# One-byte counts in the third layer of a graph network kernel

## The reference

```
x = layernorm(x + segment_sum(x[src] @ W[edge_type], dst))       # first layer
x = layernorm(x + segment_sum(x[src] * edge_weight, dst))        # second
x = layernorm(x + segment_sum(x[src], dst))                      # third
x = layernorm(x + tensor-product messages of an MLP, summed)     # fourth
```

## Time and profile before

| | us |
|---|---|
| median of three runs | 6759.45 |
| profiled execution, own time | 6756.3 |
| its span | 6754.5 |
| PE matmul busy | 5258.6 (78%) |
| PE weight loads | 4062.3 (60%) |
| DVE busy | 3937.8 (58%) |
| ACT busy | 2910.4 (43%) |
| POOL busy | 4128.8 (61%) |
| chain that ended last | POOL 59%, issue 19%, DMA 15%, PE 4% |

### The profile page before, as it was taken

How to read it: one execution, slowest core, us unless ns; L and a number is a source line. 1 busy time by engine, 2 the same in 40 slices (tenths; PEclk the granted TensorE clock), 3 DMA queues, 4 the chain that set the end, 5 groups by cost and what they waited for, 6 DMA issues and landing times.

```text
span 6754.5 us, 124961 instructions
## 1 busy us (share of the span) xinstructions
PE 5258.6 (78%) x43024; PEld 4062.3 (60%) x43025; DVE 3937.8 (58%) x7842; ACT 2910.4 (43%) x7150; POOL 4128.8 (61%) x4168
## 2 busy tenths in 40 slices
PE   6777777776777766755556769999999999999997
PEld 3367767776666666721112436777776777777766
DVE  4366666666666666620001027777777777777777
ACT  4444434343443433410000016666666666666665
POOL 0677777777777777710000027777777777777774
PEclk8555555555555555567667977787878777777877
DMA  8744444444444444489999961111111111111111
GB/s 270 265 164 175 172 164 164 173 173 164 164 164 172 175 164 164 180 325 386 387 387 378 387 211 28 27 27 27 27 27 27 27 27 28 28 28 27 27 27 20
DMA packets 512177, 1005.50 MB, mean 149 GB/s; under 512 B 180257, under 2 KB 247906, under 8 KB 478306
## 3 DMA queue, kind: packets, MB, share of 16 engines
q1 hardware_dynamic: 289890, 453.14, 19.4%
q10 hardware_dynamic: 88800, 475.02, 17.8%
q0 software_dynamic: 133120, 71.57, 6.5%
HBM read 521.51 MB, written 476.05 MB: 148 GB/s over the span
## 4 chain that ended last, share of the span: by engine, by line
POOL 59%; issue 19%; DMA 15%; PE 4%; ACT 1%; DVE 1%; POOLq 0%; SPq 0%; ACTq 0%; DVEq 0%
POOL gathered L506 59%; DMA arena<-adj 9%; DMA arena<-counts 4%; PE psum L710 2%; PE psum L884 1%; PE psum L888 1%; DMA rel_table<-arena 1%; ACT table_out L542 0%; PE psum L736 0%; PE psum L767 0%; DMA rel_table<-table_out 0%; ACT arena L542 0%; DMA arena<-in_L_gnn_weight 0%; PE psum L949 0%; DMA arena<-arena 0%
## 5 line engine op out<-in xcount | busy, mean ns | idle before, releaser
L506 POOL DMA_INDIRECT gathered<-x_rows,idx x2048 | 2065.5, 1009 | 1725.8 <-issue 1725.8
L506 POOL DMA_INDIRECT gathered<-rel_table,idx x2048 | 1998.0, 976 | 632.1 <-issue 632.1
L591 ACT COPY arena<-psum 128x512 f32<-128x512 f32 x1024 | 604.2, 590 | 1580.6 <-PE psum L817 1551.1
L949 PE MATMUL psum<-w,arena 65*128 65x256 f32 x4096 | 1231.8, 454 | 2.3 <-DVE arena L1392 2.3
L949 PEld LDWEIGHTS psum<-w,arena 65*128 65x128 f32 x4096 | 914.9, 231 | 301.3 <-issue 130.0
L817 PE MATMUL psum<-arena 64*128 64x64 bf16 (+1 forms) x12288 | 534.8, 254 | 536.7 <-DVE arena L1188 497.0
L767 PE MATMUL psum<-gathered,arena 128*128 128x32 f32 x4096 | 826.2, 380 | 150.1 <-DMA gathered<-rel_table,idx 148.1
L767 PEld LDWEIGHTS psum<-gathered,arena 128*128 128x128 f32 x4096 | 815.2, 309 | 165.1 <-issue 151.7
L767 PE MATMUL psum<-arena 128*128 128x184 f32 x4096 | 895.8, 379 | 3.4 <-DVE acc L1217 3.4
L767 PEld LDWEIGHTS psum<-arena 128*128 128x128 f32 x4096 | 861.1, 237 | 40.6 <-issue 3.9
L817 PEld LDWEIGHTS psum<-arena 64*128 64x128 bf16 x12288 | 494.1, 120 | 577.4 <-issue 561.2
(11 more groups left out here) (173 smaller groups left out, 5339.8 us busy)
## 6 DMA issues: line engine op xcount, KB each, us to landing
adj<-arena ACTq DMA_DIRECT2D x128, 2048.0 KB
arena<-adj SPq DMA_DIRECT2D x128, 2048.0 KB, 19.8
counts<-arena ACTq DMA_DIRECT2D x128, 1024.0 KB
arena<-counts SPq DMA_DIRECT2D x64, 2048.0 KB, 20.0
rel_table<-table_out ACTq DMA_DIRECT2D x16, 2048.0 KB, 7.5
rel_table<-arena ACTq DMA_DIRECT2D x16, 2048.0 KB, 7.6
gathered<-rel_table,idx POOLq DMA_INDIRECT x2048
arena<-in_edge_attr SPq DMA_DIRECT2D x128, 256.0 KB
```

The costliest lines, as they stand in the source:

```text
L506: pool.indirect_dma_start(gathered[:, s, j, :], None, rows[l], bass.IndirectOffsetOnAxis(ap=idx[:, s, j:j + 1], axis=0),).then_inc(rows_in ...
L591: act.copy(w_to, made[:, 0]).then_inc(w_out, 1)
L949: mm = pe.matmul(pair[g % 2][:, WN * q:WN * q + WN], hidden[:, s % 2, q, P * g:P * g + P], w2[:, :], start=True, stop=True)
```

## The change

`counts` is stored in one byte per entry: ACT casts to the 8-bit float format `float8e4`, the stores and loads move the bytes as `uint8`, and PE reads them as `float8e4`. A load of 2 MB then holds 32 of the 64 `high` values, so there are 32 loads. The slots are also checked for repeated sources: `prepare_slots` compares each slot's source with those 1 to 4 places further on and sums the matches in each lane and round; the dense path is taken only if no lane has more than four. The pad records get distinct sources for this. The arena shrinks by 768 columns.

```
-        counts = nc.dram_tensor("counts", [CHUNKS, P, HIS, STRIP_D], F16).ap()
+        counts = nc.dram_tensor("counts", [CHUNKS, P, HIS, STRIP_D], U8).ap()
-        ARENA = 27904
+        ARENA = 27136
+        repeats = sb("repeats", [P, ROUNDS + 1])
+        slot_same = sb("slot_same", [P, REPEATS, 2, SLOT])
-        SLOT_LINKS, TAKE_LINKS = 8, 7
+        SLOT_LINKS, TAKE_LINKS = 11, 7
# load_strips (SP)
-                matrix, his = ((adj, SUPER), (counts, 2 * SUPER))[l - 1]
+                matrix, his = ((adj, SUPER), (counts, COUNT_HI))[l - 1]      # COUNT_HI = 32
-                    to = load_in[k] if l == 1 else load_in[k].bitcast(F16)
+                    to = load_in[k] if l == 1 else load_in[k].bitcast(U8)
# strip_rows (ACT)
-                    act.copy(c_to, made[:, 1]).then_inc(c_out, 1)
+                    act.copy(c_to, made[:, 1], saturate=False).then_inc(c_out, 1)
# end of the first layer (PE)
-            pe.transpose(bank_slot[0:1, 0:P], found_col[:, :], ident[:, :]).then_inc(found_turned, 1)
+            for k in range(2):
+                pe.transpose(bank_slot[0:1, P * k:P * k + P], found_col[:, k:k + 1], ident[:, :]).then_inc(found_turned, 1)
# dense_strips (PE)
-                        part_in = load_in[at] if l == 1 else load_in[at].bitcast(F16)
+                        part_in = load_in[at] if l == 1 else load_in[at].bitcast(F8)
-                dense_strips(2, 2 * SUPER)
+                dense_strips(2, COUNT_HI)
# setup (DVE)
-            dve.memset(pad[:, :], -1.0).then_inc(packed, 1)
+            dve.memset(pad[:, 1:2], -1.0)
+            dve.tensor_scalar(pad[:, 0:1].bitcast(I32), part_i[0:SLOT, :], -1.0, -1.0, ALU.mult, ALU.add
+                              ).then_inc(packed, 1)
+            dve.memset(slot_same[:, :, :, :], 0.0)
# prepare_slots (DVE), behind its last operation
+                slots_made(dve.tensor_scalar(slot_i[:, 0], words, NODES - 1, None, ALU.bitwise_and), due(9))
+                for k in range(1, REPEATS + 1):
+                    same = dve.tensor_tensor(slot_same[:, k - 1, :, 0:SLOT - k], slot_i[:, 0, :, 0:SLOT - k],
+                                             slot_i[:, 0, :, k:SLOT], ALU.is_equal)
+                slots_made(same, due(10))
+                slots_made(dve.tensor_reduce(repeats[:, bass.ds(q, 1)],
+                                             slot_same[:, :, :, :].rearrange("p k b s -> p (k b s)"), AX.X, ALU.add), due(11))
# end of the first layer (DVE)
-            dve.tensor_reduce(found_col[:, :], found[:, 0:ROUNDS], AX.X, ALU.add).then_inc(found_ready, 1)
-            dve.wait_ge(found_turned, 1)
+            dve.tensor_reduce(found_col[:, 0:1], found[:, 0:ROUNDS], AX.X, ALU.add)
+            dve.tensor_reduce(found_col[:, 1:2], repeats[:, 0:ROUNDS], AX.X, ALU.max).then_inc(found_ready, 1)
+            dve.wait_ge(found_turned, 2)
+            link(dve.tensor_reduce(found_row[:, 1:2], bank_slot[0:1, P:2 * P], AX.X, ALU.max))
+            link(dve.tensor_scalar(found_row[:, 3:4], found_row[:, 1:2], float(REPEATS), None, ALU.is_le))
...
```

More of the change, by code:

```diff
@@ L24 @@
 LOADS = 6
+COUNT_HI = 32
+REPEATS = 4
 ALU = mybir.AluOpType
@@ L30 @@
 BF16 = mybir.dt.bfloat16
-F16 = mybir.dt.float16
+F8 = mybir.dt.float8e4
+U8 = mybir.dt.uint8
 AX = mybir.AxisListType
@@ L153, in build @@
         found = sb("found", [P, ROUNDS + 1])
-        found_row = sb("found_row", [1, P + 2])
-        found_col = sb("found_col", [P, 1])
+        found_row = sb("found_row", [1, 4])
+        found_col = sb("found_col", [P, 2])
+        repeats = sb("repeats", [P, ROUNDS + 1])
+        slot_same = sb("slot_same", [P, REPEATS, 2, SLOT])
         dense_ok = sb("dense_ok", [1, 1], I32)
@@ L171, in build @@
         stage_w = [cut(HIS * STRIP_D).rearrange("p (h d) -> p h d", d=STRIP_D) for _ in range(2)]
-        stage_c = [cut(HIS * STRIP_D // 2).bitcast(F16).rearrange("p (h d) -> p h d", d=STRIP_D) for _ in range(2)]
+        stage_c_at = [cut(HIS * STRIP_D // 4) for _ in range(2)]
+        stage_c = [a.bitcast(F8).rearrange("p (h d) -> p h d", d=STRIP_D) for a in stage_c_at]
+        stage_bytes = [a.bitcast(U8).rearrange("p (h d) -> p h d", d=STRIP_D) for a in stage_c_at]
         half_cols = HALF_D * (P + 4 * HIS) // 2
         half_at = [table_out[:, :, :].rearrange("p a b -> p (a b)")[:, 0:half_cols], cut(half_cols)]
-        assert taken[0] == ARENA - 2 * TILES * P
+        assert taken[0] <= ARENA - 2 * TILES * P
         def half_part(h, at, width):
@@ L595, in strip_rows @@
                 act.wait_ge(c_out, due(GROUPS + 2))
-                act.dma_start(counts[bass.ds(c, 1)].rearrange("a p h d -> p (a h) d"), stage_c[s % 2]).then_inc(c_stored[s % 2], 16)
+                act.dma_start(counts[bass.ds(c, 1)].rearrange("a p h d -> p (a h) d"), stage_bytes[s % 2]).then_inc(c_stored[s % 2], 16)
             for k in range(2):
@@ L635, in _ @@
             with act.If(dense):
-                strip_sums(2, HIS // (2 * SUPER))
+                strip_sums(2, HIS // COUNT_HI)
             with act.Else():
@@ L1316, in _ @@
             dve.wait_ge(strip_made, GROUPS * CHUNKS)
-            dve.tensor_reduce(found_col[:, :], found[:, 0:ROUNDS], AX.X, ALU.add).then_inc(found_ready, 1)
-            dve.wait_ge(found_turned, 1)
+            dve.tensor_reduce(found_col[:, 0:1], found[:, 0:ROUNDS], AX.X, ALU.add)
+            dve.tensor_reduce(found_col[:, 1:2], repeats[:, 0:ROUNDS], AX.X, ALU.max).then_inc(found_ready, 1)
+            dve.wait_ge(found_turned, 2)
             link(dve.tensor_reduce(found_row[:, 0:1], bank_slot[0:1, 0:P], AX.X, ALU.add))
-            link(dve.tensor_scalar(found_row[:, 1:2], found_row[:, 0:1], float(EDGES), None, ALU.is_equal))
-            dve.tensor_copy(dense_ok[:, :], found_row[:, 1:2]).then_inc(dense_known, 1)
+            link(dve.tensor_reduce(found_row[:, 1:2], bank_slot[0:1, P:2 * P], AX.X, ALU.max))
+            link(dve.tensor_scalar(found_row[:, 2:3], found_row[:, 0:1], float(EDGES), None, ALU.is_equal))
+            link(dve.tensor_scalar(found_row[:, 3:4], found_row[:, 1:2], float(REPEATS), None, ALU.is_le))
+            dve.tensor_tensor(dense_ok[:, :], found_row[:, 2:3], found_row[:, 3:4], ALU.mult).then_inc(dense_known, 1)
             normalise(0)
```

## The result

The changed kernel takes 6659.51 us (median, 6656.24 to 6661.26), beside 6759.97 for the kernel before in the same runs: a ratio of 0.985, 95% interval 0.9838 to 0.9862, so about 100 us faster. The forecast was 6672, 87 faster. The profiled execution took 6657.84 us against 6756.3, with a span of 6656.0 against 6754.5.

A forecast was written before the change was run, and what follows sets the result against it. It took POOL's gathers to bound the first layer and DMA loads the second and third. -93 (third layer) + 5 (POOL) + 1 (end of first layer) = -87 us, giving 6672; range 6655 to 6690, widened to 6715.

The forecast's parts named there:

- The third layer, -93: Third layer: half the loads end PE's waits for counts; PE then binds at 14.64 us a strip, gaining 93 us.
- A: Third layer: PE slower by clock or one-byte operand; at 0.43 us a matmul 6891 us in all; 6%.
- E: Third layer: one-byte matmuls run at twice the rate, so the loads bind; 6582 us in all; 1%.
- The DMA share "near 0.8": Third layer: a sign that the forecast is right, the DMA engines' busy share falling to near 0.8.
- POOL and the shared port, +5: First layer: VectorE's new mask and comparisons lengthen POOL's gathers by 0.16 us a round, 5 us over 32 rounds.
- Rival B: First layer: shared port lock costs POOL all 1.6 us of new work each round, 51 us, total 6718; 4%.
- VectorE's cover: First layer: 2.7 us of new work a round hides under 1.8 us of PE work and 2.1 of slack; cost 0.
- rival C: First layer: new VectorE work outgrows its 3.9 us cover; at 5 us a round it adds 35 us, 6707; 4%.
- rival D: First layer: ACT's cast to one byte is slower, delaying the scatters; up to 41 us, 6713 in all; 4%.
- End of the first layer, +1: End of first layer: extra reductions, transpose and compare delay the second layer's loads by 1.0 us.
- The fourth layer, 0: Fourth layer: the change does not touch it, so its time stays unchanged.
- Rival F: The new test of repeats rejects this data, so both middle layers are gathered; about 10,960 us in all; 0.5%.

The follow-up runs named there:

- f16_loads_twice: The kernel before, counts still f16, but 32 loads each feeding twice the matmuls, half the counts left out: 6676.12 us, ratio 0.9861.
- half_matmuls: The changed kernel with 16 of each load's 32 third-layer matmuls left out, on the slower chip: 10030.19 us.
- test_long: The changed kernel with twelve distances in the test of repeats and the comparisons made three times a round: 6723.53 us, ratio 0.9962.
- test_twelve: The changed kernel with twelve distances compared in the test of repeats in place of four: 6677.77 us, ratio 0.9864.
- bytes_alone: The changed kernel without the test of repeats, one-byte counts and 32 loads kept: 6678.99 us, ratio 0.9865.
- after_2: The changed kernel unaltered, run again beside the third set of kernels: 6652.98 us, ratio 0.9858 to the kernel before.
- before_again: The kernel before, unchanged, run and profiled a second time: 6780.26 us, ratio 1.0005.
- test_alone: The kernel before with the new test of repeats added, counts still f16 in 64 loads: 6770.40 us, ratio 0.9994.
- arena_as_before: The changed kernel with the arena at its old size of 27904 columns: 6657.92 us, ratio 0.987 to the kernel before.
- packed_2: The changed kernel with the third layer's three bf16 parts as separate 32-row matmuls in four column groups by turns, third set: 6605.45 us, ratio 0.9786.
- after_again: The changed kernel unaltered, run beside the second set on the slower chip: 10106.14 us, ratio 0.9871 to the kernel before there.

## Why the prediction was right

- **The third layer, -93.** Measured -92.3. Each link held: the one-byte matmul costs what the f16 one does (test: f16_loads_twice), the wait for `counts` went, and PE came late next (half_matmuls). Rivals A and E, a slower or a faster one-byte matmul, fell with the 13.99 us. With the rule of the Trainium skill ("TensorE: Matmul & The Clock Gate", section on the weight-path perf modes) that fp8 outside DoubleRow runs at bf16 speed, the trace agrees: 13.99 us for 64 in both types.
- **The DMA share "near 0.8"** was wrong: 0.66. Six of the 32 loads are in stock when PE starts, so only 26 x 2.1 MB fall into 237 us, the 231 GB/s of the row. The sum did not use it.
- **POOL and the shared port, +5.** Nothing of it was seen: mean 975 ns against 976 over the layer, 2619.7 us against 2620.9. In a part of the first layer (700 to 1500 us) the 20 gathers that lie beside the comparisons and reductions take 0.95 us in the mean, the other 606 take 0.98. Rival B, the lock at full price, fell. The row under the estimate, long gathers beside the wide bf16 operations, had been read as a price per microsecond of any VectorE work; it is not. The same page of the Trainium skill ("SBUF — State Buffer", "Who interferes with whom") also says, marked as inferred, that a two-input `tensor_tensor` takes the read side only while writing descriptors needs the write side. That would have given 0 for the comparisons, and I had not weighed it. It does not hold for every gather: in test_long, with thirty-six comparisons a round, some beside them take twice as long (last section).
- **VectorE's cover.** Right in its sign for this change, with 2.0 us where I had 2.7 (the mask took 0.23, not 0.42, and the comparisons 0.22 each, not 0.29), of which 0.20 is exposed. Wrong in its size: I had taken the slack of a round from the one round whose rows I read, 2.1 us, and the mean over 24.4 rounds is 112.3 / 24.4 = 4.6 us in the kernel before. So the point from which rival C counts is not 3.9 us of new work but about 1.8 + 4.6 = 6.4: test_twelve, whose exposed 2.6 us a round stay below 4.6, lost nothing that can be measured, and test_long, with 7.4 a round, lost 66.6 us. The waits alone don't give that number: (7.4 - 4.6) x 32 would be 90, the 5.3 us a round of bytes_alone would give 67, and the 3.8 of after_2, on the same chip, 113. PE's own work shrinks too: in 700 to 2700 us its matmuls take 64.5 ns each in test_long and 66.4 in after_2, about 1.6 us less a round. With it the count against after_2 closes, 7.4 - 3.8 - 1.6 = 2.0 us a round, 64 in 32; why the matmuls got shorter is open.
- **The casts, 0.** 599 ns in both; rival D fell.
- **End of the first layer, +1.** The new instructions are there, but a wait of VectorE with no data behind it, 3.8 us there before, went to the end of the second layer, where it takes 5.9. The third layer starts 6.1 us later, and the forecast had 5 + 1 for all ahead of it: the number is right by luck, its cause is not. What came was 3.1 us in the setup and 2.1 on that wait, beside about 1 us of instructions, and none of POOL's 5. The 3.1 us are no price of the change: the first gather starts at 278.5 and 281.1 us in two profiles of the kernel before, at 281.5 and 278.6 in two of the changed one.
- **The fourth layer, 0.** -14.1 in this pair of profiles, about the 15.0 by which two profiles of the kernel before differ, though the runs by number of loads leave room for a part of it. This is why the result looked better than the sum: without it the ledger gives -92.3 + 6.1 + 1.8 = -84.4, beside a forecast of -87.
- **Rival F**, data turned down by the test, did not come: both middle layers ran from the loads.
- **The range.** The forecast's own 6655 to 6690 holds the 6659.51. Widened "up to 6715" to take in rivals B to D it would still miss B's own 6718; none of the three came.

## What to carry to other kernels

Where a stage runs at the pace of its loads, halving their bytes gains up to the point at which the engine behind them binds, and that point can be read from a stretch in which stock was at hand. The slack that hides new work is a mean over many rounds, so take it from the grouped waits of the whole stage and not from one round, and take it from more than one profile, since it went from 3.2 to 5.3 us a round here. When an engine binds, look at which part of it is empty: here a quarter of PE's columns was worth another 47.5 us.

## What was not expected of the hardware

- **A wait that moves with the code.** Each kernel whose two places I read, eleven profiles, has exactly one wait of VectorE for nothing that the profile shows, ahead of `found_col` at the end of the first layer or of `xn` at the end of the second. At the first it took 3.79 and 6.45 (before, before_again), 3.77 (f16_loads_twice), 5.60 (bytes_alone) and 5.19 us (test_long); at the second 5.75 to 5.95 us in the six others (test_alone, the changed kernel twice, arena_as_before, test_twelve, packed_2). In the two programs that were profiled twice it stayed in its place, so it seems to go with the program and not with the execution, and the test's presence alone doesn't decide it, since test_long has the test. The Trainium skill ("Runtime: NRT & Kernel Launch", "Instruction fetch mechanics") says that a taken branch to a far target has to fetch its page first; that would fit, and no run here isolates it.
- **A long gather a round.** In test_long, 10 gathers of 700 to 1500 us take about 2.0 us instead of 0.94, one in each round, all beside the comparisons, while 55 of the 69 beside them take 1.0 or less. Over the whole layer 40 take 1.75 to 2.08 us, each of them beside comparisons, and test_twelve has three of about 2.0. The longest of each (ns: min/median/max), test_twelve and test_long:

```profile
L513 POOL DMA_INDIRECT gathered<-rel_table,idx x2048: 941/947/2012, 279.5 to 2908.2; - x187
L513 POOL DMA_INDIRECT gathered<-rel_table,idx x2048: 940/944/2083, 279.7 to 2934.3; - x187
```

  One microsecond more in each of the 40 is about the 35 us by which that layer's gathers grew (992 ns in the mean against 975, x 2048). The late PE does not hold them: the first comes at 282 us, ahead of PE's first scatter, and they are about as frequent in the first rounds, where the scatters are 2 to 11 us behind the gathers, as in the last, where they are about 30 behind. What singles out these 40 among the 172 gathers beside comparisons stays open.
- **One chip at 10.1 ms.** Waits of the changed kernel there (after_again), 700 to 2700 us:

```profile
PE psum L824 <- issue: 527.9, 543, 8.2
POOL gathered L513 <- DMA idx<-key_i: 874.4, 55, 17.3
```

PE waits for nothing that the profile shows, and POOL for its indices, by up to 17 us at a time; in the changed kernel's first profile the one wait is 6.8 us in all and the other is not there. The third layer's matmuls last 236.4 us on it, as on the others. The cause is open.
